# A decoder layer on one core: the third group's last normalisation in two slots, the fourth's second one behind the multiply, and the very last slot in halves

## What is computed

```python
x = _layernorm(x + attn(x))            # linear attention, 16 heads of 16, quadratic feature maps of q and k
x = _layernorm(x + xattn(x, ctx))      # long convolution with 16 filters over products of x and ctx, plus a skip
x = _layernorm(x + ffn(x))             # gated network, weights in 4-bit codes with scales
...
gate = jnp.einsum('th,nh->tn', xt, Wg)     # 2048 wide
up = jnp.einsum('th,nh->tn', xt, Wu)
gelu = jnp.tanh(0.7978845608028654 * (gate + 0.044715 * gate ** 3)) * gate * 0.5 + gate * 0.5
inter = gelu * up
out = jnp.einsum('tn,hn->th', inter, Wd)
```

## Time and profile before

| | us |
|---|---|
| median of 3 runs | 560.65 (560.31 to 561.21) |
| the profiled execution | 560.49, its span 558.7 |
| PE, TensorE's matmuls, busy | 532.1 (95% of the span) |
| DVE, VectorE, busy | 374.2 (67%) |
| ACT, ScalarE, busy | 147.3 (26%) |
| POOL, GpSimd, busy | 124.4 (22%) |
| mean granted clock of TensorE | 0.986 of full speed |

### The profile page before, as it was taken

One profiled execution on the slowest core, in us unless ns is written; L12 is line 12 of the kernel. 1 busy time (PEld: TensorE's weight loads), 2 busy tenths in 40 slices (PEclk: granted clock), 3 DMA queues, 4 the chain that ended last, 5 costly groups with the idle time before them and its releaser, 6 DMA issues.

```text
span 558.7 us, 8787 instructions
## 1 busy us (share of the span) xinstructions
PE 532.1 (95%) x3351; PEld 432.8 (77%) x3351; DVE 374.2 (67%) x782; ACT 147.3 (26%) x259; POOL 124.4 (22%) x195
## 2 busy tenths in 40 slices
PE   5999989999989999999999999999999999799993
PEld 5766777656878888766888888866888888688883
DVE  3999889977766668875455668874464777632334
ACT  3432320142442112242242111241422002223230
POOL 2100069300003444120003444120014561100001
PEclk9999899989999999999999999999999999899998
DMA  6532322121201110032001110040001100100001
GB/s 175 161 113 78 90 76 86 38 77 39 95 0 39 49 48 19 1 116 74 1 1 38 58 38 20 2 147 6 1 19 48 57 30 0 39 0 2 1 0 39
DMA packets 25258, 26.82 MB, mean 48 GB/s; under 512 B 2816, under 2 KB 22784, under 8 KB 25216
## 3 DMA queue, kind: packets, MB, share of 16 engines
q1 hardware_dynamic: 14208, 15.73, 9.5%
q10 hardware_dynamic: 10576, 8.95, 5.5%
q0 software_dynamic: 432, 1.57, 0.8%
HBM read 24.15 MB, written 2.10 MB: 47 GB/s over the span
## 4 chain that ended last, share of the span: by engine, by line
PE 81%; DVE 9%; issue 3%; DMA 3%; POOL 2%; ACT 1%; ACTq 0%; POOLq 0%; SPq 0%; DVEq 0%
PE bank L1049 17%; PE bank L1051 16%; PE bank L1050 16%; PE front_bank L1181 5%; PE front_bank L1184 4%; PE front_bank L1182 4%; PE front_bank L1118 3%; PE front_bank L1105 3%; PE front_bank L1153 3%; PE front_bank L1049 2%; PE front_bank L1050 2%; PE front_bank L1051 2%; DMA wo_sb<-in_woT 1%; PE front_bank L1129 1%; POOL ve L425 1%
## 5 line engine op out<-in xcount | busy, mean ns | idle before, releaser
L1049 PE MATMUL bank<-x2T_lo,ffn_hi 128*128 128x512 f32 x256 | 111.1, 434 | 3.5 <-DVE inter L991 2.1
L991 DVE TENSOR_TENSOR inter<-bank,inter 128x512 f32<-128x512 f32 x64 | 44.2, 690 | 90.0 <-PE bank L1051 89.7
L1051 PE MATMUL bank<-x2T_hi,ffn_hi 128*128 128x512 f32 x256 | 102.2, 399 | 0.0
L1050 PE MATMUL bank<-x2T_hi,ffn_lo 128*128 128x512 f32 x256 | 101.9, 398 | 0.0
L475 POOL TENSOR_TENSOR qbd<-qT_sb,ctxT_sb 128x256 f32<-128x256 f32 x128 | 79.0, 640 | 69.2 <-PE front_bank L1184 55.8
L425 POOL TENSOR_TENSOR ve<-ve,minus_half 128x2 f32<-128x2 f32 x24 | 17.4, 741 | 296.5 <-DVE ve L792 228.1
L649 ACT ACTIVATE inter_hi<-inter 128x512 fp32r<-128x512 f32 x64 | 40.4, 632 | 147.9 <-DVE inter L991 147.9
L1049 PE MATMUL bank<-ffn_lo,inter_hi 128*128 128x256 f32 x256 | 76.8, 300 | 1.1 <-DVE inter_lo L985 1.1
L643 ACT ACTIVATE inter<-bank 128x512 f32<-128x512 f32 x64 | 38.2, 597 | 136.0 <-PE bank L1051 135.9
L1051 PE MATMUL bank<-ffn_hi,inter_hi 128*128 128x256 f32 x256 | 72.1, 282 | 0.0
L1050 PE MATMUL bank<-ffn_hi,inter_lo 128*128 128x256 f32 x256 | 72.0, 281 | 0.0
(11 more groups left out here) (127 smaller groups left out, 779.5 us busy)
## 6 DMA issues: line engine op xcount, KB each, us to landing
toep_sb<-in_toep ACTq DMA_DIRECT2D x64, 128.0 KB, 2.1
xT_sb<-in_xT SPq DMA_DIRECT2D x4, 512.0 KB, 5.6
ctxT_sb<-in_ctxT SPq DMA_DIRECT2D x4, 512.0 KB, 4.5
x_sb<-in_x SPq DMA_DIRECT2D x4, 512.0 KB, 5.7
ctx_sb<-in_ctx SPq DMA_DIRECT2D x4, 512.0 KB, 6.6
out<-ctxT_sb POOLq DMA_DIRECT2D x3, 512.0 KB, 3.4
raw_w<-in_gate_p SPq DMA_DIRECT2D x8, 128.0 KB
raw_s<-in_gate_s SPq DMA_DIRECT2D x8, 128.0 KB
```

The costliest lines, as they stand in the source:

```text
L991: nc.vector.tensor_tensor(inter[:, n % 2, :], up_ps[:, :], inter[:, n % 2, :], ALU.mult).then_inc(inter_ready, 1)
L1049: nc.tensor.matmul(ps, w_hi, x_lo, start=start, stop=False, skip_group_check=True)
L1050: nc.tensor.matmul(ps, w_lo, x_hi, start=False, stop=False, skip_group_check=True)
L1051: return nc.tensor.matmul(ps, w_hi, x_hi, start=False, stop=stop, skip_group_check=True)
```

## The change

Three things are written in another way; nothing else is.

1. Group 2's third normalisation leaves `last_turn`. A new stage `late` does its statistics (`late 0`) behind slot 0 of group 3's network and its normalisation (`late 1`) behind slot 1. Only DVE has a function for it; POOL's powers and store stay where they stood in POOL's order and wait for DVE as before.
2. In `last_slots[15]` a `pause` stands ahead of `norm2`, so that on DVE the four normalisations follow the multiply of slot 15 instead of preceding it.
3. Slot 15 of group 3's network (`is_end`) is multiplied, rounded and subtracted in two halves of 256 tokens (`of_pair`), with three semaphores of their own, and PE's last `down` waits for one half ahead of each pair of sequences. In `finish` the two loops over pairs become one: the first pair's aggregates and `ve` stand ahead of the second pair's sum.

```diff
--- before.py
+++ after.py
@@ -180,6 +180,7 @@
             "filled", "const_ready", "pool_mask", "kv_ready", "prod_ready")
 
         last_mm, last_stored = sems("last_mm", "last_stored")
+        end_inter, end_hi, end_lo = sems("end_inter", "end_hi", "end_lo")
         rstd_ready = sems("rstd_ready1", "rstd_ready2", "rstd_ready3")
 
 
@@ -235,7 +236,7 @@
         for n in range(3):
             last_slots[10 + n] = conv[5 * n + 1:5 * n + 6]
         join = [("join", k) for k in range(6)]
-        last_slots[13], last_slots[14], last_slots[15] = join[0:3], join[3:6], [("norm2", 0)]
+        last_slots[13], last_slots[14], last_slots[15] = join[0:3], join[3:6], [pause, ("norm2", 0)]
 
         def stages(g, s, third):
 
@@ -260,6 +261,14 @@
         def x2_of(g):
 
             return x_sb if is_last(g) else x2_sb
+
+        def is_end(g, n):
+
+            return is_last(g) and n == NT - 1
+
+        def of_pair(j):
+
+            return slice(2 * j * S, 2 * (j + 1) * S)
 
         def skip_bank(g, j):
 
@@ -322,6 +331,8 @@
             turn(G - 2, G - 1, None)
             for s in range(NT):
                 slot(G - 1, None, s)
+                if s < 2:
+                    run(G - 2, [("late", s)])
             finish()
 
         def spread_waits(eng, g, u):
@@ -643,6 +654,13 @@
                 nc.scalar.activation(inter[:, n % 2, :], gate_ps[:, :], ACT.Gelu_apprx_tanh).then_inc(gelu_ready, 1)
 
             def inner_hi(g, n):
+                if is_end(g, n):
+                    act.wait_ge(down_mm, NT * g + n - 1)
+                    for j in range(2):
+                        act.wait_ge(end_inter, j + 1)
+                        nc.scalar.activation(inter_hi[:, n % 2, of_pair(j)], inter[:, n % 2, of_pair(j)], ACT.Copy)\
+                            .then_inc(end_hi, 1)
+                    return
                 count(act, inter_ready, NT, g, n + 1)
                 if n >= 2:
                     count(act, down_mm, NT, g, n - 1)
@@ -972,12 +990,25 @@
 
                 split_x2(prev)
                 total(done)
-                count(dve, y_ready[2], 2, done, 2)
-                stats(done, 2, res_sb, 0)
-                stats(done, 2, res_sb, 1)
-                normalise(done, 2, res_sb, res_sb)
+
+            def late(done, k):
+
+                if k == 0:
+                    count(dve, y_ready[2], 2, done, 2)
+                    stats(done, 2, res_sb, 0)
+                    stats(done, 2, res_sb, 1)
+                else:
+                    normalise(done, 2, res_sb, res_sb)
 
             def split(g, n):
+                if is_end(g, n):
+                    dve.wait_ge(down_mm, NT * g + n - 1)
+                    for j in range(2):
+                        dve.wait_ge(end_hi, j + 1)
+                        nc.vector.tensor_tensor(inter_lo[:, n % 2, of_pair(j)], inter[:, n % 2, of_pair(j)],
+                                                inter_hi[:, n % 2, of_pair(j)].bitcast(F32), ALU.subtract)\
+                            .then_inc(end_lo, 1)
+                    return
 
                 count(dve, ihi_ready, NT, g, n + 1)
                 if n >= 2:
@@ -988,6 +1019,11 @@
             def inner(g, n):
                 count(dve, up_mm, NT, g, n + 1)
                 count(dve, gelu_ready, NT, g, n + 1)
+                if is_end(g, n):
+                    for j in range(2):
+                        nc.vector.tensor_tensor(inter[:, n % 2, of_pair(j)], up_ps[:, of_pair(j)],
+                                                inter[:, n % 2, of_pair(j)], ALU.mult).then_inc(end_inter, 1)
+                    return
                 nc.vector.tensor_tensor(inter[:, n % 2, :], up_ps[:, :], inter[:, n % 2, :], ALU.mult).then_inc(inter_ready, 1)
 
             def finish():
@@ -1002,8 +1038,6 @@
                     dve.wait_ge(y_ready[2], 2 * g + j + 1)
                     for b in (2 * j, 2 * j + 1):
                         nc.vector.bn_stats(st[:, 2, b, :], res_sb[:, b, :]).then_inc(st_ready[2], 1)
-                for j in range(2):
-                    pair = slice(2 * j, 2 * j + 2)
                     dve.wait_ge(st_ready[2], NB * g + 2 * j + 2)
                     for b in (2 * j, 2 * j + 1):
                         nc.vector.bn_aggr(mv[:, 2, b, :], st[:, 2, b, :]).then_inc(mv_ready[2], 1)
@@ -1016,7 +1050,7 @@
                                             ALU.subtract, ALU.mult).then_inc(res_ready, 1)
 
             schedule(dve, turn, {"score": score, "squares": squares, "rms": rms, "factor": factor, "outproj": outproj, "norm": norm,
-                                 "conv": conv, "join": join, "norm2": norm2}, nothing, inner, split, unpack, finish)
+                                 "conv": conv, "join": join, "norm2": norm2, "late": late}, nothing, inner, split, unpack, finish)
 
 
         @block.tensor
@@ -1260,12 +1294,15 @@
             def down(g, n, pair_done=None):
 
                 weights_ready(g, n, 3)
-                count(pe, ihi_ready, NT, g, n + 1)
-                count(pe, ilo_ready, NT, g, n + 1)
+                if not is_end(g, n):
+                    count(pe, ihi_ready, NT, g, n + 1)
+                    count(pe, ilo_ready, NT, g, n + 1)
                 cols = slice(n // 2 * D, (n // 2 + 1) * D)
                 for b in range(NB):
                     toks = slice(b * S, (b + 1) * S)
-
+                    if is_end(g, n) and b % 2 == 0:
+                        pe.wait_ge(end_hi, b // 2 + 1)
+                        pe.wait_ge(end_lo, b // 2 + 1)
                     last = split_mm(down_ps[b // 2][:, (b % 2) * D:(b % 2 + 1) * D],
                                     inter_hi[:, n % 2, toks], inter_lo[:, n % 2, toks],
                                     ffn_hi[:, 2, n % 2, cols], ffn_lo[:, 2, n % 2, cols],
```

## The result

The changed kernel takes 554.05 us (553.06 to 556.13, 5 runs) against 560.5 (559.57 to 561.21, 5 runs) of the kernel before beside it: the ratio is 0.9888, 95% interval 0.9866 to 0.991, or 6.3 us less (5.0 to 7.5). The kernel before took 0.15 us less here than the 560.65 that the forecast starts from; 560.65 times the first ratio is 554.4, inside as well.

The account below looks back on a forecast made before the run. TensorE (PE) was taken to bound the kernel, with gains only where it stands still or runs at its lower clock. 0.53 + 2.29 + 1.63 + 0.70 + 0.20 = 5.35 us off 560.65 gives 555.3, range 554.2 to 557.2.

Parts of the forecast that it names:

- Part 1: Last turn: multiply of slot 15 ahead of norm2 on VectorE, so `down(15)` starts 0.53 us sooner.
- Part 2: Last network: third group's last normalisation in two slots, so the gap ahead of `up(1)` goes, 2.29 us.
- The clock: `up(1)` and `down(0)` of the last network: 1.63 us come back if the clock stays at 2.4 GHz.
- rival 1: The clock falls somewhere all the same, 556.9 us; chance 0.13.
- Part 3: Last slot in halves: `down(15)`'s first matmul comes 0.70 us sooner, ends 0 and 0.85.
- Rival 2: Last slot: halves bring nothing, since each pays its fixed part (0.14 us by VectorE rows), 556.0 us; chance 0.08.
- Part 4: End of program: statistics of the first pair ahead of the second sum, 0.20 us, ends 0 and 0.35.
- Rival 3: Last network: statistics only push the wait by one slot; gap 0.5 and low stretch 1.63 remain, 557.4 us; chance 0.05.
- Rival 4: Last network: normalising waits for a late POOL, PE stops at `up(3)`, clock falls; slower, 562.0 us; chance 0.02.

Follow-up runs that it names:

- e1: Kernel before with only the third group's last normalisation spread over two slots (stage `late`): 555.79 us, ratio 0.994.
- e2: Kernel before with only norm2 moved behind the multiply of slot 15: 559.01 us, ratio 0.9985.
- e11: Kernel before with matmuls that compute nothing added in the first 120 us, its gap ahead of `up(1)` left idle: 558.95 us, ratio 1.0.
- e12: Kernel before with the same early fills and 8 unused matmuls filling the gap ahead of `up(1)`: 557.8 us, ratio 0.9977.
- e3: Kernel before with only the last slot in halves, `finish` in its old order: 558.4 us, ratio 0.9974.
- e4: Kernel before with only the two loops of `finish` made one: 559.55 us, ratio 1.0001.
- e6: Changed kernel with the third group's statistics and normalisation both behind slot 0: 556.92 us, ratio to the kernel before 0.9951.
- e7: Kernel before with four more VectorE products ahead of the last network's slot 0 multiply, doubling the gap: 562.86 us, ratio 1.0061.

## Why the prediction was right

- **Part 1**, forecast 0.53 us: 0.72 (3.88 to 3.16). The mechanism was right; the length of norm2 was mis-sized, because the old 1.47 held a wait for GpSimd's second power (473.99, third tile at 474.02), and 1.29 is its length without.
- **Part 2**, forecast 2.29: the wait went, and e1 shows it alone. The price was 0.17 short: in e2, with gap and full clock, `up(1)` and `down(0)` take 2.99 us, 0.18 more than behind no gap, and the whole way 2.46 more than without the gap. What was said to be late next, was: the multiply of slot 1 at 485.40 and that of slot 2 at 488.70, both without PE waiting. The half microsecond in hand at `up(2)` was as worked out.
- **The clock**, forecast 1.63: about 1.3 on average, 0.7 to 1.9, by e11 and e12. Of 4.44 us for `up(1)` and `down(0)`, 1.45 were clock (2.99 without); the other 0.18 belong to the gap and were counted here. And the stretch isn't always there: three of five profiles with the idle gap have none (e2, e3, e4). That the low clock follows from the gap is shown by filling it while the wait stays (e12 against e11). What decides in which execution it comes isn't shown. The forecast took the stretch as certain in the kernel before; rival 1 had a stretch somewhere all the same, and there are some in the first 120 us, but in both kernels alike.
- **Part 3**, forecast 0.70: 0.61 to 0.62 (e3). The three halves take 1.27 us together, close to the 1.31 worked out; the working left out that the hand-off behind a half takes 0.10 us instead of 0.03, twice. Rival 2, halves that bring nothing, fell. Its price of 0.14 us for two halves was too high by the working's own overlap of 0.08: measured are 0.76 - 0.69 = 0.07.
- **Part 4**, forecast 0.20: 0.13 (e4); the third tile's wait is 0.26 us, where the working gave it some 0.15. The last small operation ends 3.83 us behind the first sum instead of 3.78, and the second power frees VectorE 0.82 behind its start (549.64 to 550.46) instead of 0.75.
- Rival 3 didn't come, because the work is in two slots (e6). Rival 4 has nothing for it: GpSimd took 1.34 us for the two powers (485.22 to 486.56), and VectorE got to the normalisation at 487.40.

By the profiles the path (forecast 3.72) is 0.72 + 2.46 + 0.61 + 0.13 = 3.92 us shorter, and with 1.3 for the clock 5.2. The forecast's 5.35 is as near as that partly by luck: parts 1 and 2 were 0.36 too small, parts 3 and 4 and the clock 0.5 too large. The 5.2 lies inside both intervals measured for the change, 5.0 to 7.5 and 3.7 to 5.9. That the first figure, 6.3, is above it needs no further cause: the early low stretches, which the change doesn't touch, differ from run to run, and each profile reaches the last matmul of `up(15)` between 471.3 us (e2, no low stretch ahead of it) and 474.3 (e7, two of them). They aren't all of it: e3 and e4, with one each, reach it at 471.92 and 473.47. Why a given execution has one at a given place stays open.

## What to carry to other kernels

Where one engine's queue holds a long tail of work for a finished group ahead of a short instruction that the bound engine needs, spread the tail behind that instruction, one slot at a time, and add up for each slot when the next needed instruction is due: with 1.4 us of delay on the multiply there was half a microsecond left here, and another 1.5 us in the same slot did stop TensorE (e6). An idle stretch of TensorE like this one, 2.5 us from start to start, costs its length and, often but not always, about 1.5 us of low clock behind it; one profile can't tell how often, a pair of runs with the stretch idle and filled can, if the other idle places are filled first. Where the wait can't be taken away, matmuls into an unused bank can keep the clock: in the last gap they gave 1.3 us (e12 against e11). They have to be measured at each place, since those in the first 120 us brought the kernel before nothing (e11).

## What the runs showed of the hardware

The same gap of 2.5 us was followed by a granted clock of 0.50 (1.2 GHz) in the profiles of the kernel before and of e11, and by 1.00 (2.4 GHz) in those of e2, e3 and e4. TensorE's wait of 1.48 us for GpSimd just before 77 us was followed by 1.00 before and by 0.50 in the changed kernel's profile. In e11 the clock fell only 1.4 us after TensorE had gone on (483.79, low from 485.2). The low stretches end by themselves while the matmuls go on: some 3.3 us behind the short gap, over 6 at the doubled one, where it began while TensorE still waited. Two VectorE operations of 256 elements take 0.76 us together, one of 512 takes 0.69; on ScalarE it is 0.72 against 0.63. In the last slot the next engine starts 0.10 us behind the end of a 256-element operation, and 0.03 to 0.04 behind one of 512.
